# Cross-attention and expert routing on one core: the first three steps of the pipeline put in another order

## The reference

```python
def attention(queries, keys, values):            # 16 heads of 16 channels
    q, k, v = (queries @ Wq + bq, keys @ Wk + bk, values @ Wv + bv)
    qp, kp = elu(q) + 1.0, elu(k) + 1.0
    # causal linear attention: sums over earlier tokens of kp (x) v, applied to qp
    out = scan(kp, v, qp) / cumsum(qp, axis=1)
    return out @ Wo + bo

def experts(h):                                  # 8 experts, the best one per token
    logits = relu(h @ W1 + b1) @ W2 + b2
    e = argmax(softmax(logits))
    return h @ expert_W[e] + expert_b[e]

x = x + attention(layernorm(x), ctx, ctx)
x = x + experts(layernorm(x))
```

## Time and profile before

| | us |
|---|---|
| median of 3 runs | 1118.31 (1118.07 to 1119.86) |
| the profiled execution | 1114.8 |
| its span, first to last instruction | 1113.1 |
| PE busy | 1033.8 (93%) |
| DVE busy | 875.7 (79%) |
| POOL busy | 596.5 (54%) |
| ACT busy | 458.6 (41%) |

### The profile page before, as it was taken

One profiled execution on the slowest core, in us unless ns is written; L12 is line 12 of the kernel. 1 busy time (PEld: TensorE's weight loads), 2 busy tenths in 40 slices (PEclk: granted clock), 3 DMA queues, 4 the chain that ended last, 5 costly groups with the idle time before them and its releaser, 6 DMA issues. The chain is left out here.

```text
span 1113.1 us, 38244 instructions
## 1 busy us (share of the span) xinstructions
PE 1033.8 (93%) x15980; PEld 748.6 (67%) x15980; DVE 875.7 (79%) x1908; ACT 458.6 (41%) x741; POOL 596.5 (54%) x546
## 2 busy tenths in 40 slices
PE   3899999999999999999999999999999999988584
PEld 1566666667777677777777677767667777766463
DVE  2588888887878888898888888887888889695442
ACT  1644444444444444444444444444444444421220
POOL 4143445455556655565556646545665455465755
PEclk9999999999999999999999999999999999998888
DMA  3732333342334444433334444323444433241541
GB/s 109 217 112 78 97 97 97 97 116 62 109 120 135 135 125 126 131 93 99 112 126 135 135 116 135 112 74 111 129 135 120 130 105 97 83 147 35 183 142 58
DMA packets 89387, 127.31 MB, mean 114 GB/s; under 512 B 13694, under 2 KB 68609, under 8 KB 89089
## 3 DMA queue, kind: packets, MB, share of 16 engines
q1 hardware_dynamic: 76544, 91.04, 29.5%
q0 software_dynamic: 12672, 33.84, 8.4%
HBM read 73.03 MB, written 36.06 MB: 98 GB/s over the span
## 5 line engine op out<-in xcount | busy, mean ns | idle before, releaser
L611 DVE TENSOR_TENSOR stage<-b_s,causal 128x1024 f32<-128x1024 f32 x192 | 226.2, 1220 | 35.8 <-PE b_s L920 30.9
L444 POOL DMA_INDIRECT buckets<-row,place x128 | 184.2, 1439 | 34.9 <-issue 34.9
L452 POOL DMA_INDIRECT out<-rows x136 | 136.0, 1000 | 58.8 <-issue 44.8
L461 POOL TENSOR_TENSOR onehots<-onehots,onehot 128x32 bf16<-128x32 bf16 x32 | 7.8, 243 | 246.5 <-DVE place L731 246.5
L893 PE MATMUL b_a<-xnT,wq_sb 128*128 128x512 f32 x256 | 127.6, 623 | 6.6 <-ACT x2T L543 4.3
L474 POOL TENSOR_TENSOR x_res<-x_res,bias_o 128x1024 f32<-128x1024 f32 x32 | 84.0, 2624 | 71.7 <-DMA x_res<-in_x 71.7
L893 PE MATMUL b_a<-ctxT,wk_sb 128*128 128x512 f32 x256 | 118.4, 605 | 1.8 <-ACT pos L507 1.8
L898 PE MATMUL b_b<-wo_sb,attT 128*128 128x256 f32 x512 | 118.4, 384 | 0.8 <-DVE attT L808 0.8
L898 PE MATMUL b_b<-wv_sb,ctxT 128*128 128x256 f32 x512 | 119.0, 385 | 0.0
L983 PE MATMUL b_s<-we_sb,x3T 128*128 x464 | 113.1, 389 | 1.0 <-ACT x3T L516 0.8
L898 PEld LDWEIGHTS b_b<-wv_sb,ctxT 128*128 128x128 f32 x512 | 94.7, 190 | 15.8 <-issue 0.5
(11 more groups left out here) (128 smaller groups left out, 1806.6 us busy)
## 6 DMA issues: line engine op xcount, KB each, us to landing
rows<-buckets SPq DMA_DIRECT2D x136, 130.0 KB, 5.2
x_in<-in_x SPq DMA_DIRECT2D x32, 512.0 KB, 5.2
ctxT<-in_ctx SPq DMA_DIRECT2D x32, 512.0 KB, 5.8
qsel<-qp SPq DMA_DIRECT2D x256, 64.0 KB
x_res<-in_x SPq DMA_DIRECT2D x32, 512.0 KB, 6.9
out<-rows POOLq DMA_INDIRECT x136
we_sb<-in_L_ffn_expert_W SPq DMA_DIRECT2D x8, 256.0 KB, 5.9
buckets<-row,place POOLq DMA_INDIRECT x128
```

Of the source, the lines that this page charges most:

```text
L444: pool.indirect_dma_start(buckets, bass.IndirectOffsetOnAxis(place[:, slot(route), t:t + 1], 0), row[:, slot(route), t, :], None).then_inc ...
L452: pool.indirect_dma_start(out.rearrange("t p n -> (t p) n"), bass.IndirectOffsetOnAxis(rows2[:, r, TOKEN:TOKEN + 1].bitcast(U32), 0), rows ...
L611: dve.tensor_tensor(dst.rearrange("p g h s q -> p g (h s) q"), b_s[:, :, 256 * t:256 * t + 256].rearrange("p g (a q) -> p g a q", q=C), ca ...
```

## The change

Three things are changed, all in the prologue and steps 0 to 3.

Order of work: in step 1 the keys and values of group 0 are projected (`keys_of`), ahead of its queries, and step 2 has only norm of group 1 (and the running sum of group 0). The means of `wq_sb` are multiplied between keys and values of group 0, those of `w1_sb` in the middle of step 2; DVE subtracts them there (`centre_q`, `centre_1`). DVE takes the statistics of group 1 first in step 1, and ACT makes `xn` of group 0 in step 1. Group 1 is turned in step 2 through the banks `b_b`.

Queues: wk, wv, bias_k, wq, bias_v and bias_q are issued by ACT, each with a semaphore of its own; SP issues `ctxT` and `x_in` of group 0 and `x_in` of group 1 first, then the six other weights, `ctxT` of group 1, after a wait `x_in` of group 2, and, after the `qsel` copies of group 0, the experts.

Constants: the engines wait for the first 18 of POOL's constants. The memsets of `qsel` come after the root of group 0 on POOL; the first users of `vsel` and `qsel` wait for 20 and for 22.

```diff
...
-    WEIGHTS = 16 * 14
+    WEIGHTS = 16 * 6
...
+    CONSTS = 18
     POOL_MADE = 22
-    MADE = 13
+    MADE = 11
...
+        def keys_of(j, norm, project):
+            return norm if j == 1 else None if j == 2 else project
...
-                if load:
+                if j == 0:
+                    sp.dma_start(ctxT[:, slot(load), :, :], of_ctx(load)).then_inc(s_ctx[slot(load)], 16)
+                if load and j != 2:
                     if group_no(load) >= 2:
                         sp.wait_ge(s_xn, n(load, 4, -4))
                     sp.dma_start(x_in[:, slot(load), :, :], of_x(load)).then_inc(s_x[slot(load)], 16)
-                    if group_no(load) == 0:
+                    if group_no(load) == 1:
                         load_weights()
-                if norm:
+                if j == 1:
+                    sp.dma_start(ctxT[:, slot(load), :, :], of_ctx(load)).then_inc(s_ctx[slot(load)], 16)
+                    sp.wait_ge(s_xn, 4)
+                    after = (1, 0)
+                    sp.dma_start(x_in[:, slot(after), :, :], of_x(after)).then_inc(s_x[slot(after)], 16)
+                if norm and j > 2:
                     if group_no(norm) >= 2:
                         sp.wait_ge(s_v, n(norm, 2, -2))
                     sp.dma_start(ctxT[:, slot(norm), :, :], of_ctx(norm)).then_inc(s_ctx[slot(norm)], 16)
-                    if group_no(norm) == 1:
-                        load_experts()
+                if j == 2:
+                    load_experts()
...
                     if group_no(norm) >= 2:
                         sp.wait_ge(s_sc, free)
+                    sp.wait_ge(s_const, POOL_MADE)
                     sp.wait_ge(s_qp, made)
...
             for v in range(2):
-                pool.memset(qsel[:, v, :, :, :], 0.0).then_inc(s_const, 1)
                 pool.memset(vsel[:, v, :, :, :, :], 0.0).then_inc(s_const, 1)
-            pool.wait_ge(s_wld, WEIGHTS)
...
+                if j == 0:
+                    for v in range(2):
+                        pool.memset(qsel[:, v, :, :, :], 0.0).then_inc(s_const, 1)
...
+            act.dma_start(wk_sb[:, :, :], wk.rearrange("(k p) n -> p k n", p=P)).then_inc(s_wk, 16)
+            act.dma_start(wv_sb[:, :, :], wv.rearrange("(k p) n -> p k n", p=P)).then_inc(s_wv, 16)
+            for k in range(KC):
+                act.dma_start(bias_k[:, k:k + 1], bk[P * k:P * k + P].rearrange("(p o) -> p o", o=1)).then_inc(s_bk, 16)
+            act.dma_start(wq_sb[:, :, :], wq.rearrange("(k p) n -> p k n", p=P)).then_inc(s_wq, 16)
+            act.dma_start(bias_v[:, :], bv.rearrange("(o n) -> o n", o=1).to_broadcast((P, D))).then_inc(s_bv, 16)
+            for k in range(KC):
+                act.dma_start(bias_q[:, k:k + 1], bq[P * k:P * k + P].rearrange("(p o) -> p o", o=1)).then_inc(s_bq, 16)
             act.preload_act_table_set("natural_log_exp_and_others")
-            act.wait_ge(s_wld, WEIGHTS)
+            act.wait_ge(s_const, CONSTS)
+            act.wait_ge(s_bk, 16 * KC)
...
-                if group_no(norm) >= 1:
-                    act.wait_ge(s_kp, n(norm, 2, h - 1))
+                if group_no(norm) == 0:
+                    act.wait_ge(s_bq, 16 * KC)
+                if group_no(norm) != 1:
+                    act.wait_ge(s_kp, n(norm, 2, h - 1) if group_no(norm) else h + 1)
+                else:
+                    act.wait_ge(s_qp, h + 1)
...
-                if project:
+                keys = keys_of(j, norm, project)
+                if keys:
                     for h in range(KC):
-                        act.wait_ge(s_k, n(project, 2, h + 1))
-                        act.wait_ge(s_qp, n(project, 2, h + 1))
+                        act.wait_ge(s_k, n(keys, 2, h + 1))
+                        if group_no(keys) >= 1:
+                            act.wait_ge(s_qp, n(keys, 2, h + 1))
...
                         act.activation(pos[:, h, :], b_a[:, h, :], ACT.Relu, bias=bias_k[:, h:h + 1]).then_inc(s_ke, 1)
+                if j == 1:
+                    normed(norm)
...
                     act.wait_ge(s_xnTp, n(norm, k=1))
                     if group_no(norm) >= 1:
                         act.wait_ge(s_q, n(norm, 2))
-                    act.activation(xnT[:, :, :], b_a[:, :, :], ACT.Copy).then_inc(s_xnT, 1)
+                    act.activation(xnT[:, :, :], b_b[:, :, :] if j == 2 else b_a[:, :, :], ACT.Copy).then_inc(s_xnT, 1)
+                if j == 1:
+                    normed(load)
...
+                if load and j > 1:
+                    normed(load)
...
-            dve.wait_ge(s_const, POOL_MADE)
+            dve.wait_ge(s_const, CONSTS)
...
-            dve.wait_ge(s_wld, WEIGHTS)
-            dve.wait_ge(s_wmean, 1)
-            dve.tensor_tensor(wq_sb[:, :, :], wq_sb[:, :, :],
-                              b_s[:, 0, 0:D].rearrange("p (o n) -> p o n", o=1).to_broadcast((P, KC, D)),
...
             dve.wait_ge(s_cst, MADE)
+            def centre_q():
+                dve.wait_ge(s_wmean, 1)
+                dve.tensor_tensor(wq_sb[:, :, :], wq_sb[:, :, :],
+                                  b_s[:, 0, 0:D].rearrange("p (o n) -> p o n", o=1).to_broadcast((P, KC, D)),
+                                  ALU.subtract).then_inc(s_wcent, 1)
...
+            def centre_1():
+                dve.wait_ge(s_wmean, 2)
...
             def step(j, load, norm, project, attend, merge, route):
+                if j == 1:
+                    statistics(load)
...
-                if project:
-                    dve.wait_ge(s_ke, n(project, 4, 4))
-                    dve.scalar_tensor_tensor(kp[:, slot(project), 1, :], ex[:, 1, :], 1.0, pos[:, 1, :],
+                if keys:
+                    if group_no(keys) == 0:
+                        centre_q()
+                    dve.wait_ge(s_ke, n(keys, 4, 4))
+                    dve.scalar_tensor_tensor(kp[:, slot(keys), 1, :], ex[:, 1, :], 1.0, pos[:, 1, :],
                                              ALU.min, ALU.add).then_inc(s_kp, 1)
+                    if group_no(keys) == 0:
+                        dve.wait_ge(s_const, POOL_MADE - 2)
+                        dve.wait_ge(s_bv, 16)
...
+                if j == 2:
+                    centre_1()
...
+                if load and j != 1:
+                    statistics(load)
...
-            pe.wait_ge(s_const, POOL_MADE)
-            pe.wait_ge(s_wld, WEIGHTS)
-            for k in range(KC):
-                last = pe.matmul(b_s[:, 0, 0:D], average[:, :], wq_sb[:, k, :], start=(k == 0), stop=(k == KC - 1))
-            last.then_inc(s_wmean, 1)
-            for k in range(KC):
-                last = pe.matmul(b_s[:, 1, 0:FF], average[:, :], w1_sb[:, k, :], start=(k == 0), stop=(k == KC - 1))
-            last.then_inc(s_wmean, 1)
-            pe.wait_ge(s_cst, MADE)
+            pe.wait_ge(s_const, CONSTS)
...
+            def mean_of_q():
+                pe.wait_ge(s_wq, 16)
+                for k in range(KC):
+                    last = pe.matmul(b_s[:, 0, 0:D], average[:, :], wq_sb[:, k, :], start=(k == 0), stop=(k == KC - 1))
+                last.then_inc(s_wmean, 1)
...
+            def mean_of_1():
+                pe.wait_ge(s_wld, WEIGHTS)
+                for k in range(KC):
+                    last = pe.matmul(b_s[:, 1, 0:FF], average[:, :], w1_sb[:, k, :], start=(k == 0), stop=(k == KC - 1))
+                last.then_inc(s_wmean, 1)
...
                 if attend:
+                    if group_no(attend) == 0:
+                        pe.wait_ge(s_wcent, 2)
...
+                keys_for = keys_of(j, norm, project)
+                if keys_for:
+                    a = slot(keys_for)
+                    pe.wait_ge(s_ctx[a], 16 * half(keys_for) + 16)
+                    if group_no(keys_for) == 0:
+                        pe.wait_ge(s_wk, 16)
+                    else:
+                        pe.wait_ge(s_qe, n(keys_for, 4, 4))
                     channels_first(b_a[:, 0, :], wk_sb, ctxT[:, a, :, :], 0).then_inc(s_k, 1)
                     if route:
                         pe.wait_ge(s_place, n(route, k=1))
                     channels_first(b_a[:, 1, :], wk_sb, ctxT[:, a, :, :], 1).then_inc(s_k, 1)
+                    if group_no(keys_for) == 0:
+                        mean_of_q()
+                        pe.wait_ge(s_wv, 16)
                 elif route:
...
                 if norm:
                     pe.wait_ge(s_xn, n(norm, 4, 4))
-                    if project:
-                        pe.wait_ge(s_ke, n(project, 4, 4))
-                    turned(b_a, xn).then_inc(s_xnTp, 1)
+                    if keys_for:
+                        pe.wait_ge(s_ke, n(keys_for, 4, 4))
+                    else:
+                        pe.wait_ge(s_vs, 2)
+                    turned(b_b if j == 2 else b_a, xn).then_inc(s_xnTp, 1)
...
+                    if j == 1:
+                        pe.wait_ge(s_wcent, 1)
+                    if j == 2:
+                        pe.wait_ge(s_qe, 4)
```

(41 more changed lines are left out.)

50 lines of the change are left out of this document (24 added, 26 removed).

## The result

| | before | after |
|---|---|---|
| median, us | 1119.09 (4 runs, 1118.07 to 1123.95) | 1106.55 (4 runs, 1101.64 to 1107.14) |
| profiled execution, us | 1114.8 | 1101.64 |
| its span, us | 1113.1 | 1099.9 |

The ratio is 0.9877, with a 95% interval of 0.9838 to 0.9915: 1.2% faster, between 0.9% and 1.6%. The ratio counts a fifth run of after too, 1109.18 us. The forecast was 1106.3 us, within 1103.0 to 1110.5.

The account below looks back on a forecast made before the run. PE was taken to bound the kernel, busy 1033.8 of 1113.1 us. Its earlier start and reordered work bring keys of group 1 from 45.39 to 33.4, so 1118.3 - 12.0 = 1106.3 us, range 1103.0 to 1110.5.

Parts of the forecast that it names:

- Start of PE: Kernel start: PE needs only 18 constants, wk and group 0's ctxT, so begins at 5.7 us instead of 12.31.
- the bounds of 4.2 and 8.0: Kernel start: earliest and latest time in us for PE's first work, depending on when ctxT lands.
- First keys: Group 0's keys, PE's first work: eight at the slow 0.853 us, 6.8 us in all, ending at 12.5.
- Rival B: Prologue: PE starts at 4.2 us and its clock rises sooner; 14 to 16 us gained, chance 0.09.
- qp of group 0: Step 1, after group 0's queries, Exp and Relu: qp complete at 25.2 us, where before it was 31.71.
- From qp to the first scores: SP's qsel copies, no longer covered by other work: 6.8 us to landing, PE idle from 29.9 to about 32.2.
- Keys of group 1: After the first scores: they start at 33.4 us instead of 45.39, 12.0 us sooner.
- The same distance at every mark of the middle: Long middle: the 12 us lead stays unchanged at any mark, since PE's queue moves forward as a whole.
- What is late next: SP and POOL after the prologue: x_res issued at 43.4, POOL's addition ends at 54.0, hidden with 1.3 us to spare.
- Rival C: PE's pauses at 18.3, 24.2 and 29.9 us keep it at 1.2 GHz; up to 19.5 us lost, 1125.8 us, chance 0.05.
- The weighed sentence of the Trainium skill: Weight loads: queues of different engines share transfer engines, so a second saves only issuing; otherwise PE starts 1.4 us sooner.

Follow-up runs that it names:

- qsel_and_centre: After, with half of group 0's qsel copies issued by ACT and w1 centred after the running sum; 1176.90 us on the second chip, one run.
- after_again: After itself, unaltered, timed again beside before on the second chip; ratio to before 0.9902 (0.9869 to 0.9935).
- early_apart: After, with the experts loaded in step 1 and POOL's addition held until group 1's running sum is done; ratio to before 0.987, second chip.
- after_third: After itself, unaltered, timed again on the third chip; median 1106.67 us, ratio to before 0.987 (0.9834 to 0.9906).
- one_queue: After, with the eight DMAs that ACT issued put on SP's queue behind ctxT; 1176.74 us on the second chip, one run.
- start_only: Before, with the new queues, semaphores and constants but the old order of work; 1115.49 us, one run, where before took 1120.52.

## Why the prediction was right, step by step

The total was right, 1106.3 for 1106.55, and so was the mechanism: an earlier first matmul and keys and values ahead of the queries bring the queue of matmuls forward. But two of its terms were off in opposite directions, and that they nearly cancel is luck; so is an agreement to 0.3 us in a kernel whose runs differ by more. The gain was 12.5 us between medians and 13.2 between profiled executions, for 12.0.

- Start of PE: 5.7 forecast, 5.42 measured. Right; the bounds of 4.2 and 8.0 were not needed.
- First keys: 6.8 us forecast, 5.27 measured, and 5.2 to 6.5 in the other traces. This is the step that failed first: I carried over the 7.2 us that the old start took to come to speed. In after the weight loads are 0.34 us long up to 8.11 and 0.19 from 8.81, so the pace changed 3.3 us after PE began. Rival B had named it.
- qp of group 0: 25.2 forecast, 22.72 measured, 1.5 of it from the keys, 0.3 from the start and 0.4 from the means of wq, which had been costed with a slow matmul; the rest is rounding.
- From qp to the first scores: 6.8 forecast, 7.2 measured; pause 2.3 forecast, 2.81 measured. Right, and qsel_and_centre showed that issuing makes 1.8 us of it.
- Keys of group 1: 33.4 forecast, 31.03 measured; the lead 14.4 for 12.0.
- The same distance at every mark of the middle: wrong. 3.3 us were given back in step 3, which happened to bring the lead to 11.0, near the 12.0 forecast; 1.8 of them are the stop, the rest slow matmuls behind it, and in after_again only 0.8 was given back. I had asked whether data would be late, found every transfer hidden, and not whether the traffic itself, 12 us nearer to PE's work, would hold up something that isn't data: PE's instructions. The row for it was in the trace of before, 0.81 us of "issue" at 60.50, and I passed over it.
- What is late next: right in its result. x_res was issued at 40.69 (43.4 forecast), POOL's addition ended at 51.88 (54.0 forecast) and nobody waited for it; the memsets ended at 15.0 (16 forecast). But the addition was taken at 4.39 us, from a row in which it ran beside the running sum; apart from DVE it took 2.35 (early_apart). That it slows DVE when it comes first had no term.
- Rival C, the pace falling in the pauses, is real but small: of nine traces with a pause for qsel of 2.0 us or more, it fell in five, at a cost of 1.6 us in four of them and 3.0 in after_third, not 19.5. In neither trace with fillers did it fall in that pause.
- The weighed sentence of the Trainium skill (DMA: Bandwidth & Descriptors, section Issuing engines are not separate DMA queues) holds here: one_queue starts as early as after, and in start_only the last weight landed no sooner for being issued 3.4 us sooner.

What stays open: nothing names the engine to which a packet of the queue "instruction" belongs; that it is PE's follows from the times and from the shift with the fillers. Why the first keys take 5.2 us once and 6.5 another time, and why the pace falls in one pause and not in another of the same length, isn't shown. And runs of after differ by 10 us on one chip and by 15 on the second, and the distance between two traces wanders by 2 us and more from group to group in the middle; how much of this is POOL meeting DVE's running sum (6 to 16 of the 30 sums between 60 and 1000 us took over 3 us in the ten traces off the second chip, none or one in the four on it) wasn't tried.

## What to carry to other kernels

At the start of a kernel, order decides what an early input is worth: sort the first work by what it needs, and let the engine that bounds the kernel begin with what needs least; an early start without that order gave 1.1 of 14.4 us. When a chain is moved forward, everything that lay in its shade is nearer too: look for transfers that now fall beside the bounding engine's dense stretches, for a helper engine whose operation now overlaps a critical one, and for short pauses of the bounding engine that no data explains, which may grow: set them beside the packets of the instruction queue. A pause of 2 to 3 us on TensorE cost 1.6 to 3.0 us more in slow matmuls behind it in five of nine traces, so it can be worth more to remove than its length.

## What the runs showed of the hardware

- TensorE's pace at the start: from the first matmul of the kernel, the change from 0.85 to 0.43 us from one weight load to the next came 3.3 us later in after, and over 5 us later in one_queue (a load lasts 0.33 us at 10.33, 0.19 at 10.91); first keys of the same work took 5.2 to 6.5 us. The page gave the granted clock as 1.00 throughout that stretch, while in later pauses it showed the fall (0.50 for 30 to 35 us in after_third).
- A pause of TensorE of 2.0 to 2.9 us brought the pace down in five of nine traces; one of 0.97 us did not, nor did the same pause with matmuls in it that nobody reads (two traces).
- VectorE and GpSimd: beside GpSimd's addition on 128x1024 float32, VectorE's product took 3.15 us instead of 1.22, and its running sum 4.34 instead of 2.29. In before, where the running sum had started 0.05 us earlier, it kept its 2.29 and the addition took 4.39. Whichever began second took longer, by up to 2.1 us.
- TensorE stopped for up to 2.6 us at one fixed place of its list, after 53 to 55 of 64 equal matmuls, and sooner by as many matmuls as had been put in ahead of it. It went on 2.3 to 2.5 us after a packet of the queue "instruction" (16 KB) had started, in all ten traces that stopped there. That packet started 3.5 us ahead of the place at a DMA share of 0.13 and at the place at 1.09.
